# Expert tiles of 128 rows instead of 256, second weight matrices held in SBUF, first ones through four buffers

## The chip, the core and the metric

The kernel runs on one core of a Trainium2 chip, written by hand in Bass: each of the five engines (TensorE "PE", VectorE "DVE", ScalarE "ACT", GpSimd "POOL", SyncE "SP") has its own instruction stream, and semaphores are the only order between them. The metric is the device time of one execution in microseconds (us), lower is better. Arithmetic in the part that is changed is float32, except for the ranking matmuls (bf16 one-hots).

## What is computed

Two Flamingo-style blocks on x of 8 x 512 x 256 and a context of 8 x 1601 x 256. Three parts (a cross attention, an attention with four heads chosen by a router, a cross attention of 16 heads) take nearly all of the time and are not touched. The last part is a mixture of eight experts, of which each row uses one:

```python
x_flat = x.reshape(b * t, d)                      # 4096 rows of 256, normalised
logits = x_flat @ w_gate + b_gate
probs = jax.nn.softmax(logits, axis=-1)
route_p = jnp.max(probs, axis=-1)
route_idx = jnp.argmax(probs, axis=-1)            # one of NE = 8 experts
h = jax.nn.relu(jnp.einsum('nd,edm->enm', x_flat, W1) + b1[:, None, :])   # 256 -> 1024
y = jnp.einsum('enm,emd->end', h, W2) + b2[:, None, :]                    # 1024 -> 256
out = y[route_idx, jnp.arange(n)] * route_p[:, None]
x = x + jnp.tanh(g_ffn[1]) * out
```

## The kernel before

**The first 2900 us.** A software pipeline over the eight batch items; in each, NU = 208 steps `u` place the work of three items on the engines. Each engine's stream is an unrolled loop over `b` and `u` (SP: `attend` and `fill`). The last round, b = B, finishes the last item: heads out, output projection (L1079), norm, gate (L1087). In it SP stores the item's residual (L470), its normalised rows (L474) and its gate weights (L478) to `dramR`, one row of 528 floats per token.

**The routing.** VectorE makes one-hots of the expert numbers, TensorE counts and ranks with small matmuls (L1311, L1314), and VectorE works out how many tiles each expert needs and which expert each tile belongs to: `tex`, ET integers (L1773 to L1783, signal `v_tex`). Then it makes one-hots of tile columns (L1795, `v_oht`, four pieces early and one for the last item's rows after L1801 to L1792), and TensorE multiplies them with one-hots of the ranks (L1322, 64 matmuls, the last eight for the last item) into the list of row numbers per tile (`pe_id`). VectorE turns it into gather and scatter indices (L1807, L1810, `v_id`).

**The expert stage.** The rows are sorted by expert into tiles of TS rows. As each expert's rows are padded to whole tiles, ET = 4096 / TS + 7 tiles are computed, whatever the inputs. NH = TS / 128. For each tile j:
- SP (`load_weights`, L511) waits until tile j - 2 is done (`v_y`), loads the tile's expert number into a register (L515) and issues four DMAs: first matrix (L516, 256 x 1024, 1 MB), first bias (L518), second matrix (L520, 1024 x 256, 1 MB), second bias copied to all partitions (L522). Two buffers of each.
- POOL (`fetch`, L682) gathers the tile's rows from `dramR` with one indirect DMA per 128 rows, XB = 3 tiles ahead.
- TensorE transposes the rows (`turn_rows`, L1334), VectorE copies them to SBUF (`rows_in`, L1815).
- TensorE (`hidden`, L1344) computes the hidden layer transposed: 8 blocks of 128 hidden units by 2 halves of the input; the weights are the stationary operand and the TS rows stream past. One f32 matmul in the code is two instructions in the trace. Results go to PSUM banks 2 to 5 (`h_place`); ScalarE adds bias and ReLU (L883) into `hT`, after a signal per full bank.
- TensorE (`outputs`, L1355) computes the output rows: for each 128 rows, 8 matmuls with `hT` stationary and the second matrix, 256 columns, streaming.
- VectorE (`rows_out`, L1822 and L1823) adds the bias, multiplies with the gate weight and adds the residual; POOL scatters the rows to `dramO` (L692).

TensorE's order is `turn_rows(0)`, then for every j `hidden(j)`, `turn_rows(j + 1)`, `outputs(j)`. At the end SP copies `dramO` to the output (L533).

Of the kernel before, what the change touches and what calls it, by code (L numbers as in the profile page):

```python
# [8 lines left out]
F32 = mybir.dt.float32  # L9
# [3 lines left out]
ALU = mybir.AluOpType  # L13
# [3 lines left out]
B, S, C, D = 8, 512, 1601, 256  # L17
P = 128
QT = S // P
KD = D // P  # L20
CT = -(-C // P)
# [9 lines left out]
GH = 4  # L31
# [12 lines left out]
FM = FF // P  # L44
TOK = B * S
NT = TOK // P
TS = 256
ET = TOK // TS + NE - 1
NH = TS // P
NJ = ET * NH  # L50
TE = NT - QT
RW = 2 * D + 16
XB = 3
MASKED = -float(2.0 ** 100)

MB, F0, F1, F2, SB, VB = (0, 1), 2, 3, 4, (5, 6), 7
# [83 lines left out]
def flamingo(nc, a):  # L140
    ctx_stack = ExitStack()
    with ctx_stack:
        def sem(name):
            return ctx_stack.enter_context(nc.semaphore(name))
# [55 lines left out]
        def carve(region, size):  # L200
            at = [0]

            def take(dims, dt, parts=P):
                n = int(np.prod(dims)) * (4 if dt in (F32, I32, U32) else 2)
                words = -(-n // 4)
                ap = region[0:parts, at[0]:at[0] + words]
                at[0] += words
                assert at[0] <= size, (at[0], size)
                if dt is not F32:
                    ap = ap.bitcast(dt)  # L210
                if dt in (BF16,) and words * 2 != int(np.prod(dims)):
                    ap = ap[:, 0:int(np.prod(dims))]
                names = "abcd"[:len(dims)]
                if len(dims) > 1:
                    ap = ap.rearrange(f"p ({' '.join(names)}) -> p {' '.join(names)}",
                                      **{k: v for k, v in zip(names, dims)})
                return ap
            return take
# [75 lines left out]
        spare = take([1], F32)  # L294

        take = carve(regC, R - R_AB)
        hT = take([FM, TS], F32)
        ys = [take([NH, D], F32) for _ in range(2)]
        w1 = [take([KD, FF], F32) for _ in range(2)]
        w2 = [take([FM, D], F32) for _ in range(2)]  # L300
        b1 = [take([FM], F32) for _ in range(2)]
        b2 = [take([D], F32) for _ in range(2)]
        xs = [take([NH, RW], F32) for _ in range(XB)]
        xsT = [take([KD, TS], F32) for _ in range(2)]

# [41 lines left out]

        g_late, v_oh, pe_rank, v_tex, v_ohr, v_oht, pe_id, v_id = (
            sem(n) for n in ("g_late", "v_oh", "pe_rank", "v_tex", "v_ohr", "v_oht", "pe_id", "v_id"))
        w_loaded = [sem(f"w_loaded{i}") for i in range(2)]  # L350
        xs_loaded = [sem(f"xs_loaded{i}") for i in range(XB)]
        pe_xsT, v_xsT, pe_h, a_h, pe_y, v_y = (sem(n) for n in ("pe_xsT", "v_xsT", "pe_h", "a_h", "pe_y", "v_y"))
        ys_stored = [sem(f"ys_stored{i}") for i in range(2)]
# [8 lines left out]
        def _(sp):  # L362
# [101 lines left out]

            def fill(b, u):
                n, e = b + 1, b - 1
                if e >= 0:
                    if u == 21:
                        sp.wait_ge(v_oC, QT * (e + 1))
                        sp.dma_start(dramR[S * e:S * (e + 1), D:2 * D].rearrange("(t p) n -> p t n", p=P), xc  # L470
                                     ).then_inc(x_stored, 16)
                    if u == 28:
                        sp.wait_ge(v_xn, 4 * norm_d(e) + 4)
                        sp.dma_start(dramR[S * e:S * (e + 1), 0:D].rearrange("(t p) n -> p t n", p=P), xn  # L474
                                     ).then_inc(n_stored, 16)
                    if u == U_GATE + 8:
                        sp.wait_ge(v_wt, e + 1)
                        sp.dma_start(dramR[S * e:S * (e + 1), 2 * D:RW].rearrange("(t p) n -> p t n", p=P), w16[:]  # L478
                                     ).then_inc(w_stored, 16)
                if n < B:  # L480
                    for i in range(VP):
                        if u == U_V[i] + 2:
                            store_v(n, i)
                    if u == U_RL + 4:
                        gather_heads(n)
                    if u == U_QC[0] + 5:
                        store_q(n, 0)
                    if u == U_QC[0] + 8:
                        load_q(n, 0)
                    if u == 153:  # L490
                        store_q(n, 1)
                    for i in range(2 * NCH):
                        if u == U_K[i] + 3:
                            store_k(n, i)
# [14 lines left out]
                                         ).then_inc(ld["ones"], 16)  # L509

            def load_weights(j):  # L511
                par = j % 2
                if j >= 2:
                    sp.wait_ge(v_y, NH * (j - 1))
                e = sp.value_load(tex[0:1, j:j + 1], min_val=0, max_val=NE - 1)  # L515
                sp.dma_start(w1[par], a["D_W1"][bass.ds(e, 1)].rearrange("o (k p) f -> p (o k) f", p=P)  # L516
                             ).then_inc(w_loaded[par], 16)
                sp.dma_start(b1[par], a["D_b1"][bass.ds(e, 1)].rearrange("o p m -> (o p) m")  # L518
                             ).then_inc(w_loaded[par], 16)
                sp.dma_start(w2[par], a["D_W2"][bass.ds(e, 1)].rearrange("o (k p) n -> p (o k) n", p=P)  # L520
                             ).then_inc(w_loaded[par], 16)
                sp.dma_start(b2[par], a["D_b2"][bass.ds(e, 1)].rearrange("o n -> (o n)").partition_broadcast(P)  # L522
                             ).then_inc(w_loaded[par], 16)

            sp.wait_ge(n_stored, 16 * B)
            sp.wait_ge(x_stored, 16 * B)
            sp.wait_ge(v_tex, 1)
            for j in range(ET):
                load_weights(j)
# [178 lines left out]
        def _(act):  # L708
# [166 lines left out]
                        start_next(b + 2, u)  # L875

            def hidden(j):
                par = j % 2
                act.wait_ge(w_loaded[par], 64 * (j // 2 + 1))
                for m in range(FM):  # L880
                    bank, at = h_place(j, m)
                    act.wait_ge(pe_h, HBK * j + m // (FM // HBK) + 1)
                    act.activation(hT[:, m, :], PS[:, bank, at:at + TS], ACT.Relu,  # L883
                                   bias=b1[par][:, m:m + 1]).then_inc(a_h, 1)
# [6 lines left out]
        def _(pe):  # L891
# [421 lines left out]
            for i in range(QT):  # L1313
                last = mm(PS[:, 0, QT * NE:(QT + 1) * NE], onesD, oh[:, TE + i, :], start=i == 0, stop=i == QT - 1)  # L1314
            last.then_inc(pe_rank, 1)
            for i in range(NT):
                if i % 7 == 0 and i < TE:
                    pe.wait_ge(v_oht, i // 7 + 1)
                if i == TE:
                    pe.wait_ge(v_oht, 5)  # L1320
                for k in range(2):
                    last = mm(PS[:, 1, 0:NJ], ohr[k][:, i, :], oht[:, i, :], start=i == 0 and k == 0,  # L1322
                              stop=i == NT - 1 and k == 1)
# [12 lines left out]
                last.then_inc(pe_xsT, 1)  # L1336

            def hidden(j):
                pe.wait_ge(w_loaded[j % 2], 64 * (j // 2 + 1))
                pe.wait_ge(v_xsT, j + 1)  # L1340
                for m in range(FM):
                    bank, at = h_place(j, m)
                    for kk in range(KD):
                        last = mm(PS[:, bank, at:at + TS], w1[j % 2][:, kk, m * P:(m + 1) * P], xsT[j % 2][:, kk, :],  # L1344
                                  start=kk == 0, stop=kk == KD - 1)
                    if (m + 1) % (FM // HBK) == 0:
                        last.then_inc(pe_h, 1)

            def outputs(j):
                for t in range(NH):  # L1350
                    past(pe, v_y, NH * j + t - 1)
                    for m in range(FM):
                        if t == 0:
                            pe.wait_ge(a_h, FM * j + m + 1)
                        last = mm(PS[:, 6 + (NH * j + t) % 2, 0:D], hT[:, m, t * P:(t + 1) * P], w2[j % 2][:, m, :],  # L1355
                                  start=m == 0, stop=m == FM - 1)
                    last.then_inc(pe_y, 1)

            turn_rows(0)
            for j in range(ET):  # L1360
                hidden(j)
# [6 lines left out]
        def _(dve):  # L1368
# [322 lines left out]
            def alone(ins):  # L1691
                ins.then_inc(*own.tick())
                dve.wait_ge(v_self, own.now())
# [123 lines left out]
            def rows_out(j):  # L1817
                par = j % 2
                past(dve, ys_stored[par], 16 * NH * (j // 2))
                for t in range(NH):  # L1820
                    dve.wait_ge(pe_y, NH * j + t + 1)
                    alone(v.tensor_tensor(ys[par][:, t, :], PS[:, 6 + (NH * j + t) % 2, 0:D], b2[par], ALU.add))  # L1822
                    v.scalar_tensor_tensor(out=ys[par][:, t, :], in0=ys[par][:, t, :],  # L1823
                                           scalar=xs[j % XB][:, t, 2 * D:2 * D + 1], in1=xs[j % XB][:, t, D:2 * D],
                                           op0=ALU.mult, op1=ALU.add).then_inc(v_y, 1)
# [64 lines left out]
```

## Time and profile before

| | us |
|---|---|
| median of the runs | 3290.82 |
| lowest and highest of three runs | 3289.27, 3303.54 |
| the profiled execution | 3308.77 |
| its span, first to last instruction | 3307.0 |
| mean granted TensorE clock, share of full | 0.937 |

Rows of the trace give the start of a piece or an instruction in us from the span's start, and its duration. PE is TensorE's matmul, PEld its weight loads, which can run beside matmuls. "xN" is a number of instructions. The duration of a single matmul is counted from start to the modelled end of its pipeline; the distance of two starts tells its pace better. A name with q (SPq, PEldq) is an engine's sequencer.

### The profile page before, as it was taken

To read this page: it belongs to the slowest core of one execution; us is meant where nothing else is said; L and a number is where in the kernel's file an instruction comes from. 1 tells how busy PE (TensorE), PEld (TensorE's weight loads), DVE (VectorE), ACT (ScalarE), POOL (GpSimd) and SP (SyncE) were. 2 spreads that over 40 slices of the span, in tenths; PEclk is the share of its full clock that TensorE was granted. 3 is DMA by queue.
4 is the path that set the end of the run, shared out by engine and by line. 5 is a ranking of instruction groups with operands and counts; after the bars stand their busy time and mean duration, and the time that the engine had idled before them with its cause. 6 is when DMAs were issued, how large, how long until landed. Compare 5 with 4: busy or idle time off the path is not lost.

```text
span 3307.0 us, 38212 instructions
## 1 busy us (share of the span) xinstructions
PE 2877.2 (87%) x13236; PEld 1331.4 (40%) x13236; DVE 1719.2 (52%) x4156; ACT 1459.8 (44%) x2794; POOL 316.6 (10%) x364
## 2 busy tenths in 40 slices
PE   5758988998899888998899889988998888859997
PEld 3423423353334333443344334433343322148886
DVE  1335556556555656555655565555555676621111
ACT  2122454545454555445454545454545555612221
POOL 0110001010100100010101010101010000012221
PEclk7878998999899999999999999998999999969999
DMA  4124212322232214220323032303221121026665
GB/s 156 54 70 110 56 34 77 88 61 50 70 94 55 64 36 119 55 74 28 99 69 80 16 119 62 82 20 119 63 63 33 53 55 36 8 90 220 219 208 175
DMA packets 190687, 267.58 MB, mean 81 GB/s; under 512 B 47813, under 2 KB 159661, under 8 KB 190358
## 3 DMA queue, kind: packets, MB, share of 16 engines
q1 hardware_dynamic: 173084, 189.97, 21.3%
q0 software_dynamic: 17408, 75.13, 6.7%
q8 instruction: 107, 1.75, 0.2%
q14 instruction: 88, 0.72, 0.1%
HBM read 203.24 MB, written 65.61 MB: 81 GB/s over the span
## 4 chain that ended last, share of the span: by engine, by line
PE 72%; DVE 15%; ACT 5%; issue 4%; SPq 3%; DMA 1%; POOL 0%; ACTq 0%; POOLq 0%; DVEq 0%
PE PS L1233 12%; PE PS L1184 10%; DVE mxC L1655 9%; PE PS L1216 7%; PE PS L953 6%; PE PS L929 5%; PE PS L1344 5%; PE PS L1355 5%; PE PS L1019 2%; PE PS L1099 2%; PE PS L1036 2%; PE PS L1029 2%; PE PS L976 2%; DVE nmB L1494 1%; PE PS L940 1%
## 5 line engine op out<-in xcount | busy, mean ns | idle before, releaser
L860 ACT ACTIVATE reg<-PS 128x512 f32<-128x512 f32 (+1 forms) x1664 | 970.3, 598 | 1205.2 <-PE PS L1216 1201.9
L1655 DVE TENSOR_REDUCE mxC<-PS 128x1 f32<-128x400 f32 (+1 forms) x2048 | 1090.1, 569 | 752.9 <-PE PS L1184 743.2
L1184 PE MATMUL PS<-reg 96*128 96x400 bf16 (+1 forms) x2048 | 693.0, 351 | 176.5 <-DVE mxC L1655 155.7
L1216 PE MATMUL PS<-reg 99*128 99x512 bf16 (+1 forms) x1664 | 642.5, 396 | 32.5 <-ACT reg L860 27.1
L1184 PEld LDWEIGHTS PS<-reg 96*128 96x128 bf16 x2048 | 203.1, 99 | 725.0 <-DVE mxC L1655 598.9
L1233 PE MATMUL PS<-reg 128*17 128x512 f32 (+1 forms) x3328 | 461.8, 628 | 0.0
L1216 PEld LDWEIGHTS PS<-reg 99*128 99x128 bf16 (+1 forms) x1664 | 165.6, 102 | 348.5 <-ACT reg L860 159.1
L929 PE MATMUL PS<-reg 128*128 128x512 f32 (+1 forms) x512 | 206.0, 526 | 1.2 <-ACT reg L756 0.7
L883 ACT ACTIVATE reg<-PS,reg 128x256 f32<-128x256 f32 x184 | 77.3, 471 | 271.0 <-PE PS L1344 271.0
L953 PE MATMUL PS<-reg 128*128 128x512 f32 (+1 forms) x416 | 193.1, 598 | 0.4 <-ACT reg L728 0.4
L1344 PE MATMUL PS<-reg 128*128 128x256 f32 x736 | 165.4, 382 | 0.9 <-DVE reg L1815 0.9
L1355 PE MATMUL PS<-reg 128*128 128x256 f32 x736 | 163.3, 379 | 0.0
L1344 PEld LDWEIGHTS PS<-reg 128*128 128x128 f32 x736 | 140.6, 191 | 22.1 <-issue 1.2
L1355 PEld LDWEIGHTS PS<-reg 128*128 128x128 f32 x736 | 137.5, 189 | 19.1
L1029 PE MATMUL PS<-ident,reg 128*128 128x128 f32 x512 | 93.6, 312 | 52.0 <-ACT reg L751 52.0
L929 PEld LDWEIGHTS PS<-reg 128*128 128x128 f32 x512 | 89.6, 195 | 77.5 <-issue 65.6
L559 POOL DMA_DIRECT2D reg<-in_A_mask x32 | 17.9, 562 | 1028.0 <-PE PS L1036 638.5
L1029 PEld LDWEIGHTS PS<-ident,reg 128*128 128x128 f32 x512 | 65.2, 158 | 124.0 <-issue 116.8
L1424 DVE CUSTOM_DVE_ANT_0 reg<-PS,reg 128x512 f32<-128x512 f32 (+1 forms) x128 | 72.4, 568 | 74.0 <-PE PS L929 68.9
L976 PE MATMUL PS<-reg,wkC 128*128 128x400 f32 (+1 forms) x256 | 107.3, 546 | 0.7 <-DVE reg L1486 0.7
L953 PEld LDWEIGHTS PS<-reg 128*128 128x128 f32 (+1 forms) x416 | 78.1, 192 | 73.4 <-issue 67.1
L1494 DVE TENSOR_REDUCE nmB<-PS 128x1 f32<-128x512 f32 x128 | 82.0, 682 | 45.9 <-PE PS L1019 45.9
(202 smaller groups left out, 2614.7 us busy)
## 6 DMA issues: line engine op xcount, KB each, us to landing
reg<-in_D_W SPq DMA_DIRECT2D x46, 1024.0 KB, 7.5
reg<-in_A_mask POOLq DMA_DIRECT2D x32, 800.5 KB, 4.8
dramK<-reg SPq DMA_DIRECT2D x144, 100.0 KB
dramV<-reg SPq DMA_DIRECT2D x48, 272.0 KB, 2.1
reg<-in_ctxT POOLq DMA_DIRECT2D x8, 1601.0 KB, 8.3
reg<-in_ctx POOLq DMA_DIRECT2D x8, 1536.0 KB, 8.1
dramQ<-reg SPq DMA_DIRECT2D x96, 128.0 KB
reg<-dramQ SPq DMA_DIRECT2D x32, 384.0 KB, 5.8
```

Of the source, the lines that this page charges most:

```text
L860: act.activation(pr[u % RING][0:r, :], PS[0:r, s_bank(g, v), :], ACT.Exp).then_inc(a_expC, 1)
L929: last = mm(PS[:, FB[i % 2], 0:w], qgA[:, k, t * P:(t + 1) * P], ctxT[:, k, c0:c0 + w], start=k == 0, stop=k == KD - 1)
L953: last = mm(PS[:, FB[m], :], ctxN[0:r, c, m * P:(m + 1) * P], ptA[0:r, c, :], start=c == 0, stop=c == CT - 1)
L976: last = mm(PS[:, FB[u % 2], 0:w], wkC[:, k, m * P:(m + 1) * P], ctxT[:, k, c0:c0 + w], start=k == 0, stop=k == KD - 1)
L1029: last = tr(PS[:, F2, k * P:(k + 1) * P], pB[i % 4][:, k * P:(k + 1) * P], ident[:])
L1184: last = mm(PS[:, bank, 0:w], qs[(NG * bb + g) % 3][0:ROWS, h, t * P:(t + 1) * P], ks[g % 2][0:ROWS, h, c0:c0 + w], start=True, stop=True)
L1216: last = mm(PS[0:r, bank, :], ks[g % 2][0:STK, h, c * P:c * P + r], qs[(NG * b + g) % 3][0:STK, h, :], start=True, stop=not with_mask)
L1233: last = mm(PS[32 * h:32 * h + DC + 1, VB, :], vc[0:r, c, g * GH + h, :], pr[(UN * g + GH * c + h) % RING][0:r, :], start=c == 0, stop=c = ...
L1344: last = mm(PS[:, bank, at:at + TS], w1[j % 2][:, kk, m * P:(m + 1) * P], xsT[j % 2][:, kk, :], start=kk == 0, stop=kk == KD - 1)
L1355: last = mm(PS[:, 6 + (NH * j + t) % 2, 0:D], hT[:, m, t * P:(t + 1) * P], w2[j % 2][:, m, :], start=m == 0, stop=m == FM - 1)
L1494: v.tensor_reduce(nmB[:, i:i + 1], PS[:, (F0, F1)[h], :], AX.X, ALU.max, negate=True).then_inc(v_nmB, 1)
L1655: v.tensor_reduce(mxC[:, h, t, j:j + 1], PS[:, MB[i % 2], 0:M_CH[j][1]], AX.X, ALU.max).then_inc(v_mx, 1)
```

## The change

- TS goes from 256 to 128: 39 tiles of 128 rows instead of 23 of 256, NH from 2 to 1, one gather and one scatter per tile. XB, the row buffers, goes from 3 to 4.
- The second matrices of all eight experts are loaded into one SBUF tensor with eight 1 MB DMAs. They stand in SP's stream at b = B, u = 6, behind a wait for the last attention product. SP waits for them to land before the first `load_weights`, TensorE before the first `turn_rows`.
- TensorE loads the expert numbers of all 39 tiles into registers, in five calls of up to eight, behind a wait for `v_tex` and ahead of the L1322 matmuls. The matmuls of `outputs` read the second matrix at an address computed from the register.
- First matrices and the two biases go through WB = 4 buffers. `load_weights` waits for tile j - 4 and issues three DMAs; before the third tile's it waits for the rows of the second.

```diff
-TS = 256
+TS = 128
-XB = 3
+XB = 4
+WB = 4
...
         take = carve(regC, R - R_AB)
+        w2 = take([NE, FM, D], F32)
+        assert NE * FM * D <= 2 * GH * C + 3 * GH * S // 2 + RING * S + CT * S // 2
+        w1 = [take([KD, FF], F32) for _ in range(WB)]
         hT = take([FM, TS], F32)
         ys = [take([NH, D], F32) for _ in range(2)]
-        w1 = [take([KD, FF], F32) for _ in range(2)]
-        w2 = [take([FM, D], F32) for _ in range(2)]
-        b1 = [take([FM], F32) for _ in range(2)]
-        b2 = [take([D], F32) for _ in range(2)]
+        b1 = [take([FM], F32) for _ in range(WB)]
+        b2 = [take([D], F32) for _ in range(WB)]
...
             def fill(b, u):
                 n, e = b + 1, b - 1
+                if b == B and u == 6:
+                    sp.wait_ge(pe_pv, UN * B)
+                    for i in range(NE):
+                        sp.dma_start(w2[:, i, :, :], a["D_W2"][i].rearrange("(k p) n -> p k n", p=P)
+                                     ).then_inc(w2_loaded, 16)
...
             def load_weights(j):
-                par = j % 2
-                if j >= 2:
-                    sp.wait_ge(v_y, NH * (j - 1))
+                par = j % WB
+                if j >= WB:
+                    sp.wait_ge(v_y, NH * (j - WB + 1))
+                if j == 2:
+                    sp.wait_ge(xs_loaded[1], 16 * NH)
...
-                sp.dma_start(w2[par], a["D_W2"][bass.ds(e, 1)].rearrange("o (k p) n -> p (o k) n", p=P)
-                             ).then_inc(w_loaded[par], 16)
...
+            sp.wait_ge(w2_loaded, 16 * NE)
             sp.wait_ge(v_tex, 1)
...
             last.then_inc(pe_rank, 1)
+            pe.wait_ge(v_tex, 1)
+            chosen = []
+            for j in range(0, ET, 8):
+                _, some = nc.values_load_multi_w_load_instructions(
+                    tex[0:1, j:min(j + 8, ET)], engines=[mybir.EngineType.PE], min_val=0, max_val=NE - 1,
+                    skip_runtime_bounds_check_because="the vector engine takes the minimum with NE - 1")
+                chosen += some
...
-                        last = mm(PS[:, 6 + (NH * j + t) % 2, 0:D], hT[:, m, t * P:(t + 1) * P], w2[j % 2][:, m, :],
+                        last = mm(PS[:, 6 + (NH * j + t) % 2, 0:D], hT[:, m, t * P:(t + 1) * P],
+                                  w2[:, bass.ds(chosen[j], 1), m, :].rearrange("p o n -> p (o n)"),
                                   start=m == 0, stop=m == FM - 1)
                     last.then_inc(pe_y, 1)
 
+            pe.wait_ge(w2_loaded, 16 * NE)
             turn_rows(0)
```

## Rows read from the trace of the kernel before

**Rows 1.** The page's first line.

```profile
span 3307.0 us, 38212 instructions
```

**Rows 2.** Windows: from, to, length, busy time by engine, clock, DMA share, GB/s.

```profile
3000.00:3050.00 50.00, 50.00 (x238) 43.70 (x237) 8.45 (x17) 12.18 (x30) 15.01 (x16) 1.00 0.62 201
```

**Rows 3.** Chain that ended last, expert stage: start us, us, what.

```profile
2954.25 1.13 PE PS L1334 x4
2956.24 9.21 PE PS L1344 x32
...
3001.43 6.93 PE PS L1344 x32
3008.80 6.94 PE PS L1355 x32
3015.74 6.93 PE PS L1344 x32
...
3280.30 3.48 PE PS L1355 x16
```

**Rows 4.** Timeline of TensorE around one tile's transposes.

```profile
3251.53 0.60 PE L1334 MATMUL PS<-ident,reg 128*128 128x128 f32 x4
3251.96 0.82 PE L1355 MATMUL PS<-reg 128*128 128x256 f32 x3
```

**Rows 5.** The same chain, a gate of an earlier item, at full clock.

```profile
2738.56 1.69 PE PS L1087 x16
```

**Rows 6.** Groups by line and shape: count, busy us, mean ns, idle before.

```profile
L883 ACT ACTIVATE reg<-PS,reg 128x256 f32<-128x256 f32 x184 | 77.3, 471 | 271.0 <-PE PS L1344 271.0
L1815 DVE COPY reg<-PS 128x512 f32<-128x512 f32 x23 | 15.9, 692 | 154.0 <-PE PS L1334 154.0
```

**Rows 7.** Timeline of the hand-over, from the routing to the first gather.

```profile
2936.27 0.35 DVE L1780 TENSOR_TENSOR reg<-reg 128x184 f32<-128x184 f32 x1
...
2937.03 0.18 DVE L1783 TENSOR_SCALAR reg<-reg 128x23 int32<-128x23 f32 x1
...
2938.25 0.40 SPq L516 DMA_DIRECT2D reg<-in_D_W  x1
...
2938.93 2.33 PE L1322 MATMUL PS<-reg 128*128 128x46 bf16 x56 [4.26 <-DVE reg L1795]
...
2941.08 0.38 SPq L516 DMA_DIRECT2D reg<-in_D_W  x1
...
2944.76 0.49 PE L1322 MATMUL PS<-reg 128*128 128x46 bf16 x8 [3.49 <-DVE reg L1795]
...
2946.43 1.10 POOL L682 DMA_INDIRECT reg<-dramR,reg  x1 [23.53 <-DVE reg L1810]
```

**Rows 8.** Timeline, last attention products and last store.

```profile
2899.85 1.92 PE L1233 MATMUL PS<-reg 128*17 128x512 f32 x16
...
2934.01 0.36 SPq L478 DMA_DIRECT2D dramR<-w  x1
```

**Rows 9.** Windows, columns as rows 2, while loads and gathers fill the DMA engines.

```profile
2950.00:2955.00 5.00, 0.75 (x4) 0.71 (x4) 0.00 (x0) 0.00 (x0) 2.88 (x4) 0.50 1.07 373
```

**Rows 10.** DMA issues, KB each, median us to landing (two stretches, 2860 to 2975 and 3000 to 3200).

```profile
dramR<-reg SPq DMA_DIRECT2D x2, 512.0 KB, 3.0
...
dramO<-reg POOLq DMA_INDIRECT x29, 2.7
reg<-dramR,reg POOLq DMA_INDIRECT x28, 6.8
```

**Rows 11.** Sequencer instructions of two lines: duration ns min, median, max.

```profile
L1299 PEldq TENSOR_LOAD <-mflag x1: 487/487/487, 248.2 to 248.2; - x1
L1299 PEldq FUSED_REGOPS  x1: 168/168/168, 248.8 to 248.8; - x1
...
L516 SPq FUSED_REGOPS  x19: 42/42/42, 3003.3 to 3260.6; - x19
```

**Rows 12.** Timeline of TensorE at that register load.

```profile
248.23 3.78 PE L916 MATMUL PS<-reg,gA 128*128 128x512 f32 x4 [0.69 <-ACT reg L714]
```

More of the change, by code:

```diff
@@ L349, in flamingo @@
             sem(n) for n in ("g_late", "v_oh", "pe_rank", "v_tex", "v_ohr", "v_oht", "pe_id", "v_id"))
-        w_loaded = [sem(f"w_loaded{i}") for i in range(2)]
+        w_loaded = [sem(f"w_loaded{i}") for i in range(WB)]
+        w2_loaded = sem("w2_loaded")
         xs_loaded = [sem(f"xs_loaded{i}") for i in range(XB)]
@@ L877, in hidden @@
             def hidden(j):
-                par = j % 2
-                act.wait_ge(w_loaded[par], 64 * (j // 2 + 1))
+                par = j % WB
+                act.wait_ge(w_loaded[par], 48 * (j // WB + 1))
                 for m in range(FM):
@@ L1338, in hidden @@
             def hidden(j):
-                pe.wait_ge(w_loaded[j % 2], 64 * (j // 2 + 1))
+                pe.wait_ge(w_loaded[j % WB], 48 * (j // WB + 1))
                 pe.wait_ge(v_xsT, j + 1)
@@ L1343, in hidden @@
                     for kk in range(KD):
-                        last = mm(PS[:, bank, at:at + TS], w1[j % 2][:, kk, m * P:(m + 1) * P], xsT[j % 2][:, kk, :],
+                        last = mm(PS[:, bank, at:at + TS], w1[j % WB][:, kk, m * P:(m + 1) * P], xsT[j % 2][:, kk, :],
                                   start=kk == 0, stop=kk == KD - 1)
@@ L1821, in rows_out @@
                     dve.wait_ge(pe_y, NH * j + t + 1)
-                    alone(v.tensor_tensor(ys[par][:, t, :], PS[:, 6 + (NH * j + t) % 2, 0:D], b2[par], ALU.add))
+                    alone(v.tensor_tensor(ys[par][:, t, :], PS[:, 6 + (NH * j + t) % 2, 0:D], b2[j % WB], ALU.add))
                     v.scalar_tensor_tensor(out=ys[par][:, t, :], in0=ys[par][:, t, :],
```

## The prediction

> **What bounds the kernel now.** I read the page first. One core runs for 3307.0 us [rows 1]. The windows come next: outside the last stage the three engines share the work, while in the expert stage TensorE is busy for all of each 50 us at granted clock 1.00 (the 2.4 GHz level), VectorE for 8.45, ScalarE for 12.18, and the DMA engines for 0.62 of their time at 201 GB/s [rows 2]. Only this stage and the hand-over before it are touched, so the 2900 us before it stay. Third, the chain that ended last. From the first tile to the last output it is TensorE alone, 32 first-layer instructions in 6.93 us, then 32 second-layer ones in 6.94, and one tile follows the other after 3015.74 - 3001.43 = 14.31 us [rows 3]. The small gap behind the first layer is the transposes of the next tile's rows. 23 such tiles make 329 us, near the stage's own 3280.30 + 6.94 - 2956.24 = 331.0 (the chain's last piece leaves TensorE halfway); the other 2 us are the first tile, whose first layer took 9.21 us behind a slow-clock stretch [rows 3]. Fewer TensorE columns here shorten the kernel one for one, as long as nothing else becomes the limit.
>
> **Smaller tiles.** Rows are padded to whole tiles per expert, and the worst case is computed always: 23 tiles of 256 rows (5888) become 32 + 7 = 39 of 128 (4992). An f32 matmul is two instructions here (16 in the code, 32 in the row).
> - Second layer: same shape per instruction (stationary 128x128, moving 256), 16 per tile instead of 32. 6.94 / 32 = 0.217 us each, so 16 take 3.47.
> - First layer: still 32 instructions a tile, each with 128 moving columns instead of 256, and each still with its own weight load. This is the price that decides. Half the columns give 0.108 us. The weight load must then fit beside it: the gate's 16 instructions of 8 columns, which can hardly be anything but weight loads, take 1.69 us, 0.106 each [rows 5]. Whether load and stream overlap at 128 columns is seen at the transposes: four of 128x128 start 3251.53, and the next layer starts 3251.96, 0.43 us for four, 0.108 each, with their loads in it [rows 4]. So 32 x 0.108 = 3.47 us.
> - Transposes: two instead of four, 0.22.
> A tile takes 3.47 + 3.47 + 0.22 = 7.16 us, and 39 take 279.2 against 329.0: **-49.8 us**.
>
> That rests on overlap. The Trainium skill ("TensorE: Matmul & The Clock Gate", Back-to-back issue gap) says that a stream of load and matmul pairs runs slower than the isolated gap where the moving side is short, 81 ns against 56 at 128 columns. The transposes here don't show that. By its ratio, 1.45, the first layer would take 5.0 us, and the sum for the tiles would be +10 instead of -50.
>
> **What must hide behind 7.16 us.** ScalarE: eight ReLUs a tile at 0.471 us for 256 columns [rows 6]; even at that price 3.8 us, and the first four can start when half the first layer is done, 1.7 us before TensorE is through it; TensorE asks for the fifth 1.7 us into the second layer. I cost it at nothing. VectorE: a copy of half the columns that took 0.692 us [rows 6] and two operations on 256 columns, under 2 us. POOL: one gather and one scatter, some 1 us each, as often per row as before. Gathers land in 6.8 us and scatters in 2.7 [rows 10]; a gather is issued some 15 us ahead, a scatter has two tiles (14 us). DMA: per tile 1.05 MB first matrix, 0.13 MB bias rows, 0.27 MB gathered, 0.13 scattered, 1.58 MB in 7.16 us = 221 GB/s, where a stretch of this trace moves 373 [rows 9]. The second matrix, a third of the old bytes, is gone from the loop, so this stays covered; if it fell to 186 GB/s the tile would be 8.5 us and the loop's gain zero. SP took 2941.08 - 2938.25 = 2.83 us for a register load and four DMAs [rows 7]; three are less, and they wait only for the tile four back, a lead of three tiles.
>
> **Second matrices loaded once.** Eight 1 MB DMAs are put in SP's queue after the last attention product, which ends at 2899.85 + 1.92 = 2901.8 [rows 8], ahead of SP's three stores of the last batch, of which the last is issued at 2934.01 [rows 8]. DMA is idle meanwhile. 8.4 MB at 373 GB/s is 22.5 us: landed by about 2925. The two earlier stores (issued near 2920 and 2924) may queue a few us; nobody needs them before the gather at 2946.43 [rows 7]. The other bound is the rate of one 512 KB store, 0.52 MB in 3.0 us, 175 GB/s [rows 10]: 48 us, landed at 2950. SP now waits for it before the first expert load, now at 2938.25 [rows 7], and TensorE before the first tile, so that would cost about 5 to 8 us. I take the first (many large transfers in flight, like the stretch of rows 9) and cost it at nothing.
>
> **Register loads.** TensorE now reads 39 expert numbers, in five calls of up to eight, between the tile table (L1783, ready 2937.03 + 0.18 = 2937.21) and the 64 ranking matmuls, queued right behind. These wait for VectorE: 56 start at 2938.93 and take 2.33 us, and the last eight can't start before 2944.76 [rows 7]. So 2944.76 - 2937.21 - 2.33 = 5.2 us are free. One load of one value on TensorE took 0.487 us, and its arithmetic 0.168 [rows 11]. Ends: 5 x 0.487 = 2.4 us (nothing on the path) and 39 x 0.655 = 25.5 (20 us on the path). I take five calls and no cost, but keep the other end. The skill's page "Runtime: NRT & Kernel Launch" (Instruction fetch mechanics) gives some 200 ns per register even in bulk; 39 would be 7.8 us and the sum 2.6 us worse; no row here shows a bulk load.
>
> **Computed addresses.** Each second-layer matmul may need register instructions on TensorE's sequencer; SP's take 0.042 us before a DMA, the one on TensorE took 0.168 [rows 11]. One or two of them per matmul are 0.04 to 0.34 us, beside 2 x 0.217 = 0.434 us of matmul. The sequencer ran that one at 248.8, while matmuls that began at 248.23 ran on for 3.78 us [rows 12], so it works beside them: nothing.
>
> **The hand-over.** VectorE's table operations get wider: L1780 took 0.35 us for 184 columns [rows 7] and gets 312, its neighbour L1774 gets 256 for 128. Four such operations widen by some 0.1 us each (an estimate, less than in proportion), and the narrower one-hots give part back: +0.2. Then it gets better. Before, the first two gathers shared the engines with four 1 MB loads and TensorE began at 2954.25, 7.8 us after POOL. Now only 2.4 MB are ahead, done about 2946, the third load waits for the second gather, and the first tile needs one gather. With the scatters' 2.7 us [rows 10] and POOL's 1, it starts 3.5 us after POOL: about -4.4 with the 0.2 in it. Two transposes and a half-size copy save 0.6 of the 1.99 us up to the first layer. Together **-4.8 us**. If contention stays, this is only -1.
>
> **Sum**: -49.8 - 4.8 = -54.6. The tail after the last output is unchanged. The profiled execution took 3308.77 us (span plus 1.8), 18 above the median 3290.82 of the runs, so 3254 for that one and **3236 us** by the median.
>
> **Rivals.**
> A. TensorE's register loads are serial, each of 39 at full price: the ranking is late by up to 20 us. For: only a single-value load is in the trace, at 0.487. Against: five calls. 3236 + 20 = 3256. If both this and the slow second-matrix load hold, 3262. Chance 0.14.
> B. Slower than before: the sequencer can't feed the second layer. Place: the eight matmuls of each tile; price: four or more register instructions of 0.168 before each, 0.67 us, plus waits that keep it from running ahead. From 0.434 + 54.6 / 312 = 0.61 us per matmul on the change loses. At 0.434 + 0.24 the time is 3236 + 75 = 3311. For: no such matmul is in the trace. Against: 0.042 on SP, and run-ahead at 248.8. Chance 0.05.
> C. Load and stream don't overlap fully at 128 columns: if half of the 0.106 us load stays outside, 39 x 32 x 0.053 = 66 us more, 3302, no difference that can be told (all of it outside would be 3368). For: only four such instructions stand in a row anywhere. Against: their 0.108 [rows 4]. Chance 0.05. The ratio of the skill's page named above would put it at 3296.
> D. Part of either, 0.12 us per first-layer instruction or a stall of some 0.4 us per tile (ReLU late, register work): 3236 + 16 = 3252. Chance 0.14.
> Forecast: 0.62.
>
> **Numbers.** Range 3222 to 3266: down for a faster load of the second matrices or a spread of the runs, up to hold A, and D with the 13 us by which the slowest run shown lies above the median; outside are B and C. A measurement tells 0.5%, 16 us, from no change. Faster 0.90 (forecast, A, D), same 0.05 (C), slower 0.05 (B).
>
> **What would show it.** The chain should have pieces of 3.47 us x32 and x16, tile spacing 7.16; second-layer spacing above 0.217 is B, first-layer above 0.11 is C. L1322's last eight should still start near 2945 (else A); the first tile near 2950; the second matrices landed before 2934; DMA share near 0.6 and no wait for w1 or rows. A loop at 7.16 with an equal total would mean the start-up went wrong.

## The result, and the profile after

| | before | after |
|---|---|---|
| median of 4 runs, us | 3292.14 | 3251.07 |
| lowest and highest, us | 3289.27, 3303.54 | 3246.73, 3263.43 |
| span of the profiled execution, us | 3307.0 | 3261.7 |
| store of the gate weights to first layer of the first tile, us | 22.2 | 21.9 |
| first layer of the first tile to the end, us | 350.8 | 305.1 |

The changed kernel takes 0.9875 of the time of before, 95% interval 0.9839 to 0.9911: 41 us less, clear of noise, and inside the predicted 3222 to 3266, but 15 us above the 3236 that was expected. The last two rows of the table tell more than the medians. The 2900 us ahead of the change carry the same code and still differ by up to 21 us between executions (SP's store of the gate weights is issued between 2913.9 and 2934.7 us in the traces of this study). So stages are measured here from the issue of that store ([rows 8], 2934.01 before) to the end of the span: 373.0 us before, 327.0 after, 326.8 in a second profile of the changed kernel. By this measure the change is worth 46.0 us. The two profiles of the changed kernel agree within 0.2; the kernel before was profiled once.

The expert stage, the chain that ended last (answers to [rows 3]):

```profile
2956.65 5.95 PE PS L1360 x32
2962.82 3.47 PE PS L1371 x16
2966.29 3.57 PE PS L1360 x32
2970.07 3.47 PE PS L1371 x16
2973.55 3.57 PE PS L1360 x32
...
3227.64 3.57 PE PS L1360 x32
```

L1360 is the first layer, L1371 the second. A tile follows the other after 2973.55 - 2966.29 = 7.26 us, where 7.16 was expected. The second layer is exact. The first takes 3.57 instead of 3.47. Nothing stands between the pieces but the 0.22 us of the transposes.

The hand-over, from SP's loads of the kept matrices to the first tile (timeline, answers to [rows 7, 8]):

```profile
2900.55 1.91 PE L1242 MATMUL PS<-reg 128*17 128x512 f32 x16
...
2902.58 17.40 SPq L473 DMA_DIRECT2D reg<-in_D_W  x8
...
2934.72 0.36 SPq L486 DMA_DIRECT2D dramR<-w  x1
...
2938.27 0.18 DVE L1801 TENSOR_SCALAR reg<-reg 128x39 int32<-128x39 f32 x1
...
2945.40 0.32 DVE L1813 TENSOR_TENSOR reg<-reg 128x156 bf16<-128x156 f32 x1
...
2948.25 2.29 PE L1338 MATMUL PS<-reg 128*128 128x39 bf16 x64 [12.88 <-issue]
...
2951.73 1.10 POOL L691 DMA_INDIRECT reg<-dramR,reg  x1 [28.12 <-DVE reg L1828]
...
2955.38 0.66 PE L1350 MATMUL PS<-ident,reg 128*128 128x128 f32 x2 [4.83 <-DMA reg<-dramR,reg]
```

The reader is to see three things. The eight loads are issued in 17.4 us and delay nothing that anyone waits for; from the end of the last attention product (2900.55 + 1.91) to the store of the gate weights it is 32.3 us, before it was 32.2. The 64 ranking matmuls (L1338) no longer run as 56 and 8 behind VectorE: all start at 2948.25, with "issue" as what ended the idle time, 2.5 us after VectorE's last one-hots were there (2945.40 + 0.32). And from POOL's first gather to the first transposes it is 3.65 us; it was 7.8 before [rows 3, 7]. What held the ranking is TensorE's sequencer (rows of L1328, ns, and where the first and the last start):

```profile
L1328 PEldq TENSOR_LOAD <-reg x5: 1702/1930/1951, 2938.5 to 2946.5; - x5
```

Five bulk loads one behind the other, 1.93 us for eight values and 1.70 for seven: 0.24 us a value. From 2938.5 to 2946.5 + 1.7 = 2948.2 TensorE started no matmul.

Windows of the expert stage (answers to [rows 2]):

```profile
3000.00:3050.00 50.00, 50.00 (x348) 46.99 (x348) 8.96 (x21) 15.15 (x54) 13.71 (x14) 1.00 0.66 219
```

TensorE is busy for all of it, at the same granted clock of 1.00, and the DMA engines move 219 GB/s where 221 was worked out.

### The profile page after: what moved, and what is told of

Its sections match the earlier page's. It is cut to its first block, busy times and chain, and to the rows that moved or that the text cites. A ratio compares the mean times of both kernels' runs of the same rounds, so it can differ in the third digit from the quotient of the medians.

```text
span 3261.7 us, 39651 instructions
## 1 busy us (share of the span) xinstructions
PE 2831.2 (87%) x13622; PEld 1308.7 (40%) x13622; DVE 1714.2 (53%) x4158; ACT 1469.5 (45%) x2922; POOL 302.7 (9%) x350
## 3 DMA queue, kind: packets, MB, share of 16 engines
q1 hardware_dynamic: 166444, 193.18, 21.9%
## 4 chain that ended last, share of the span: by engine, by line
PE 71%; DVE 15%; ACT 5%; issue 4%; SPq 3%; DMA 1%; POOL 0%; ACTq 0%; POOLq 0%; DVEq 0%
PE PS L1242 12%; PE PS L1193 10%; DVE mxC L1673 9%; PE PS L1225 7%; PE PS L962 6%; PE PS L938 5%; PE PS L1360 4%; PE PS L1371 4%; PE PS L1028 2%; PE PS L1108 2%; PE PS L1045 2%; PE PS L1038 2%; PE PS L985 2%; DVE nmB L1512 1%; PE PS L949 1%
## 5 line engine op out<-in xcount | busy, mean ns | idle before, releaser
L892 ACT ACTIVATE reg<-PS,reg 128x128 f32<-128x128 f32 x312 | 89.0, 368 | 217.0 <-PE PS L1360 217.0
L1360 PEld LDWEIGHTS PS<-reg 128*128 128x128 f32 x1248 | 147.4, 194 | 3.1 <-issue 1.0
L1360 PE MATMUL PS<-reg 128*128 128x128 f32 x1248 | 147.8, 277 | 0.6 <-DVE reg L1833 0.6
L1371 PE MATMUL PS<-reg 128*128 x624 | 141.7, 379 | 0.0
L1371 PEld LDWEIGHTS PS<-reg 128*128 128x128 f32 x624 | 115.1, 189 | 15.1
L938 PEld LDWEIGHTS PS<-reg 128*128 128x128 f32 x512 | 89.3, 194 | 77.0 <-issue 65.0
L568 POOL DMA_DIRECT2D reg<-in_A_mask x32 | 17.9, 562 | 1026.8 <-PE PS L1045 635.7
```

The lines of the kernel that those rows point to most:

```text
L938: last = mm(PS[:, FB[i % 2], 0:w], qgA[:, k, t * P:(t + 1) * P], ctxT[:, k, c0:c0 + w], start=k == 0, stop=k == KD - 1)
L1360: last = mm(PS[:, bank, at:at + TS], w1[j % WB][:, kk, m * P:(m + 1) * P], xsT[j % 2][:, kk, :], start=kk == 0, stop=kk == KD - 1)
```

## The experiments

Where a ratio stands the run was timed against the kernel before; all are compared by stage. The columns are us of the profiled execution, and "store to end" is the measure above. Each kernel but the changed one was profiled once, and the four without a ratio (fixed address, two buffers, no wait for the second gather, tile size alone) were run only for that profile.

| run | store to first layer | first layer to end | store to end |
|---|---|---|---|
| before | 22.2 | 350.8 | 373.0 |
| changed kernel | 21.9 | 305.1 | 327.0 |
| late loads | 17.9 | 307.8 | 325.7 |
| fixed address, no register loads | 17.7 | 305.6 | 323.2 |
| small tiles, all weights streamed, four buffers | 21.0 | 305.4 | 326.4 |
| kept matrices, tiles of 256 | 20.3 | 349.2 | 369.4 |
| two buffers | 21.8 | 333.5 | 355.3 |
| no wait for the second gather | 24.2 | 305.2 | 329.4 |
| loads by four | 18.1 | 305.4 | 323.5 |
| tile size alone | 21.1 | 434.9 | 455.9 |
| streamed, wait for the first gather | 17.5 | 306.8 | 324.3 |

**The changed kernel once more.**

> The changed kernel once more, as the yardstick of this chip. Expected: ratio near 0.9875, tiles 7.26 us apart, ranking matmuls 2.5 us or so after VectorE's last one-hots, first layer 54.2 us after the end of the last attention product.

Ratio 0.9889 (0.9855 to 0.9923), tiles 7.26 us apart, first layer 21.90 us after the store. The stages repeat to 0.2 us; the medians don't, to 5.

**What the register loads cost: loads placed later.**

```diff
-            for j in range(0, ET, 8):
+            def choose(j):
...
             pe.wait_ge(w2_loaded, 16 * NE)
+            choose(0)
             turn_rows(0)
             for j in range(ET):
                 hidden(j)
                 if j + 1 < ET:
                     turn_rows(j + 1)
+                if j and j % 8 == 0:
+                    choose(j)
                 outputs(j)
```

> The expert numbers are loaded into TensorE's registers later: the first eight after the ranking matmuls, while the first gather is on its way, the others eight at a time between first and second layer of tiles 8, 16, 24 and 32. Theory (the five bulk loads of 1.9 us stood in front of the ranking and pushed it back 4.3 us, and the sequencer can load registers while the array works off queued matmuls): first layer about 50 us after the last attention product instead of 54.2, tile pace unchanged at 7.26, total 4 us less than the changed kernel (ratio to the kernel before about 0.986). Rival (a load stalls the array wherever it stands): 4 us won at the start, and 4 x 1.9 = 7.7 us given back in the loop, total 3 us more than the changed kernel. Rival (the start is bound by the gather behind the weights, not by the ranking): no change.

Both the theory and half of the rival came true. The first layer starts 4.1 us earlier, so the loads had been on the path, which refutes "the start is bound by the gather". But from the first layer to the end it is 2.8 us longer, with four waits at the second layer (waits of TensorE, then the second layer of tile 8 in the chain):

```profile
PE PS L1373 <- ACT reg L892: 1.6, 4, 0.5
```

```profile
3009.83 3.73 PE PS L1373 x16
```

The columns of the first are total, times and longest, us. The waits are put down to ScalarE, whose first four ReLUs were done at 3008.6; what ended last there is the load, which started at 3007.2 and took some 2.3 us. A second layer behind such a wait also takes 3.73 us instead of 3.47. Together the four loads push the tiles back by 0.74, 0.69, 0.74 and 0.48 us, 2.65 in all (distances of the starts of second layers), and the first tile's first layer adds 0.3, 6.28 us against 5.95. That is the 2.8 within 0.2. The rival had four times 1.9 us. Ratio 0.9854 (0.9811 to 0.9898): no difference from the changed kernel that the timed runs can tell; the stages give 1.3 us.

**Do computed addresses cost anything?**

```diff
-                                  w2[:, bass.ds(chosen[j], 1), m, :].rearrange("p o n -> p (o n)"),
+                                  w2[:, j % NE, m, :],
```

and the register loads are gone. So the tiles don't take the second matrix of their expert, and the output is not the reference's; the work of each tile is the same.

> No register loads on TensorE at all, and the second layer reads the second matrix of expert j modulo 8 at a fixed address, so the output differs from the reference in which second matrix a tile uses. Theory (computed addresses cost nothing, the 0.1115 us of a first-layer instruction is the array's own pace): second layer 0.217 us and first layer 0.1115 us per instruction as in the changed kernel, first layer starts about 50 us after the last attention product. Rival (register work slows the loop): first layer back at 0.108 us, tile 7.16 us, 4 us less in the loop on top of the start.

The chain of this kernel (L1354 first layer, L1344 transposes, L1365 second layer):

```profile
3101.22 3.47 PE PS L1365 x16
3104.69 3.57 PE PS L1354 x32
3108.26 0.22 PE PS L1344 x2
3108.48 3.47 PE PS L1365 x16
```

Still 7.26 us, to the hundredth. Computed addresses cost nothing, and the 0.1 us of the first layer is not register work. Without any register load the first tile starts 4.2 us earlier; its first layer takes 6.39 us instead of 5.95, which leaves 3.8 us.

**The tile size, with all weights streamed through four buffers.** Both matrices are loaded for each tile, w2 in four buffers like w1; no kept matrices, no registers. SP's wait for the second gather before the third tile's loads stays.

```diff
+        w2 = [take([FM, D], F32) for _ in range(WB)]
...
+                sp.dma_start(w2[par], a["D_W2"][bass.ds(e, 1)].rearrange("o (k p) n -> p (o k) n", p=P)
+                             ).then_inc(w_loaded[par], 16)
...
+                                  w2[j % WB][:, m, :],
```

> Tiles of 128 rows and four buffers, but both matrices of a tile are loaded for it, as before; nothing is kept, no registers on TensorE. Per tile 2.63 MB. Theory (DMA would have become the limit, which is what the kept matrices are for): at the 348 GB/s at which the eight kept matrices were loaded, 7.56 us a tile, TensorE waits for weights, loop 295 us instead of 285, and the first layer starts some 4 us later than with an undisturbed gather; total 5 to 20 us above the changed kernel. Rival (the prefetch over four tiles is enough, kept matrices bring nothing): tiles 7.26 us apart, total that of the changed kernel or 4 us less, since the register loads are gone.

The theory falls, and the rival is right. Windows of this kernel, from, to, length, busy by engine, clock, DMA share, GB/s:

```profile
3000.00:3050.00 50.00, 50.00 (x348) 47.01 (x347) 9.35 (x21) 16.01 (x56) 13.71 (x14) 1.00 1.05 364
3100.00:3150.00 50.00, 50.00 (x346) 46.93 (x346) 9.16 (x21) 15.67 (x55) 13.30 (x14) 1.00 1.05 367
```

The DMA engines are busy for the whole stage, at 356 to 367 GB/s in the four windows from 3000 to 3200, and TensorE never waits for weights: 2.63 MB in 7.26 us is 362 GB/s. So in the loop, with four buffers, the kept matrices bring nothing. 362 is what the loop asks for and not quite what the engines can give: with the same bytes per tile the last run below moves 373 to 375. At the start the kept matrices save the first gather from waiting behind 4 MB of weights (TensorE's idle time, L1339 transposes):

```profile
2939.44 0.69 PE L1339 MATMUL PS<-ident,reg 128*128 128x128 f32 x2 [8.21 <-DMA reg<-dramR,reg]
```

From POOL's gather at 2932.41 to these it is 7.0 us against 3.65, and that is about what the register loads cost on the other side. Ratio 0.9872 (0.9842 to 0.9902): the time of the changed kernel.

**Kept matrices, tiles of 256 rows.**

```diff
-TS = 128
+TS = 256
-XB = 4
+XB = 3
```

> Second matrices kept and four buffers, but tiles of 256 rows as before (23 tiles, three bulk register loads). Theory (the loop is bound by TensorE's columns, all of the gain is the tile size): tiles 14.3 us apart, loop 331 us as before; three loads take 5.7 us against 5.2 free, so the start is 0 to 4 us better than before through the undisturbed gather; ratio 0.998 to 1.001. Rival (part of the gain is the saved weight traffic): loop shorter than 331 us.

Ratio 0.9989 (0.9970 to 1.0009), no difference. The loop has its old pace:

```profile
2961.28 6.93 PE PS L1360 x32
2968.65 6.94 PE PS L1371 x32
2975.59 6.93 PE PS L1360 x32
```

So the kept matrices and the four buffers give nothing in the loop at this tile size. By the stages the kernel is 3.6 us better than before. 2.0 are at the start: from POOL's first gather to the first transposes it is 5.5 us (2937.89 to 2943.39) instead of 7.8, and the three register loads (5.6 us) make that gather 0.4 us later. 0.7 more are the first layer of the first tile, 8.56 us against 9.21, and the rest is behind the last product. The other 42.4 us of the 46.0 come only with the small tiles.

**Two buffers instead of four.**

```diff
-WB = 4
+WB = 2
...
-                if j == 2:
-                    sp.wait_ge(xs_loaded[1], 16 * NH)
```

> As the changed kernel, with two instead of four buffers for first matrices and biases, and without SP's wait for the second gather (with two buffers it would come before a wait that holds it anyway). Theory: the load for a tile is issued about 1.8 us after the tile before last ends and lands 5.5 us later, 7.3 us against a tile of 7.26, so TensorE waits up to 1 us at each first layer: tile 7.3 to 8.2 us, loop 3 to 35 us longer. Rival (one tile of lead is enough): tile 7.26 us and the same time.

28 us slower than with four, near the upper end of the 3 to 35 that were expected. TensorE waits 26 times for 21.2 us in all, and a first layer behind such a wait takes 3.84 us instead of 3.57. One turn of its chain:

```profile
3103.86 3.48 PE PS L1369 x16
3107.44 0.43 DVE reg L1838
3107.90 0.50 DVE reg L1839
...
3109.15 0.39 SPq L524
3109.72 0.69 SPq L526
3110.59 5.27 DMA reg<-in_D_b
3115.90 3.84 PE PS L1358 x32
```

The way from the end of a tile (3107.34) over VectorE and SP's three issues to the landing of the last small load (3115.86) is 8.5 us, longer than the 7.26 us of the tile between. With tiles of 256 the same way had 14.3 us.

**The tile size alone.** The streamed kernel with two buffers. Four row buffers (XB) stay, where the kernel before has three; no run tells what that is worth.

```diff
-WB = 4
+WB = 2
...
-                if j == 2:
-                    sp.wait_ge(xs_loaded[1], 16 * NH)
```

> Tiles of 128 rows and nothing else: both matrices of a tile are loaded for it, through two buffers as before. Theory (the lead of two buffers is the issue: a buffer is free 2 us after the tile before last, four DMAs are issued in about 1.6 us and land 7.4 to 9.5 us later, so 11 to 13 us from the end of tile j - 2 to the start of tile j, and two tiles take that plus 7.26): 9.2 to 10.2 us a tile, loop 360 to 400 us, 30 to 60 us slower than the kernel before. Rival (DMA throughput is enough, so the buffers hardly matter): 7.3 to 7.8 us a tile.

83 us slower than before by the stages; the one execution took 3381.41 us. The mechanism is the expected one, the size was underrated (9.2 to 10.2 us a tile and 30 to 60 us in all were expected). One turn of the chain:

```profile
3119.86 3.48 PE PS L1358 x16
3123.43 0.44 DVE reg L1826
3123.89 0.50 DVE reg L1827
...
3126.12 0.38 SPq L522
3126.68 8.06 DMA reg<-in_D_b
3134.78 5.33 PE PS L1347 x32
3140.33 3.48 PE PS L1358 x16
3143.91 0.44 DVE reg L1826
```

Two tiles take 20.5 us here (3119.86 to 3140.33); over the stage pairs take 20.4 to 23.5, 21.4 in the mean, 10.7 a tile. From the end of a tile (3123.34) to landed weights (3134.74) it is 11.4 us, of which TensorE spends 7.3 on the tile between. Then it stands still (waits of TensorE):

```profile
PE PS L1347 <- DMA reg<-in_D_b: 89.6, 20, 6.1
```

The part that was not expected is the first layer's 5.33 us instead of 3.57. The granted clock of these stretches shows its cause (windows, columns as [rows 2]: the wait, the 3 us behind it, the next 2 us):

```profile
3130.60:3134.70 4.10, 0.00 (x0) 0.00 (x0) 0.91 (x2) 0.00 (x0) 1.96 (x2) 0.98 1.04 324
3134.80:3137.80 3.00, 3.00 (x14) 3.00 (x15) 0.00 (x0) 0.00 (x0) 0.00 (x0) 0.50 1.02 399
3138.00:3140.00 2.00, 2.00 (x20) 2.00 (x20) 0.00 (x0) 1.14 (x4) 0.00 (x0) 1.00 1.06 361
```

After a stand-still of 4.2 us (3130.6 to 3134.8) the first layer begins at 0.50, the 1.2 GHz level, 14 instructions in 3 us, and is back at 1.00 from 3138.0 on, 20 in 2 us. First layers behind a wait take 5.27 to 6.75 us, 5.7 in the mean of the 18 in the chain. So the 129.5 us that two buffers cost here against four are 89.6 of waits and, for nearly all of the rest, slow clock behind them: 20 x 2.1 = 42 by the mean (an estimate, 2 us more than is there).

**The wait for the second gather.** Four tiles' weights issued at once.

```diff
-                if j == 2:
-                    sp.wait_ge(xs_loaded[1], 16 * NH)
```

> As the changed kernel, without SP's wait for the second gather before the third tile's weights, so that four 1 MB loads are issued at once. Theory (the first gather is held up by bulk loads in the DMA queues): from POOL's first gather to the first transposes 3.65 us becomes 5 to 8 us, total 2 to 4 us more. Since the register loads have moved POOL's gather 4 us back, most of the four loads may be through by then; then only 0 to 1 us more. Rival (gathers don't suffer from loads): 3.65 us stays.

```profile
2949.73 0.66 PE L1348 MATMUL PS<-ident,reg 128*128 128x128 f32 x2 [6.97 <-DMA reg<-dramR,reg]
```

From POOL's gather at 2943.94 it is 5.8 us instead of 3.65, the first layer 2.2 us later, and 2.4 us more to the end. The gather does suffer, and the wait in the change is worth 2.2 us. The 0 to 1 us that the expectation held possible, should the loads be through by then, did not come.

**Loads by four.** As the late loads, with the calls of four values before the second layer of every fourth tile.

> As the late loads, but four expert numbers at a time, before the second layer of every fourth tile. The late loads by eight left waits of 0.4 us at four tiles and, with a slower first tile, 2.8 us more from the first layer to the end. Theory (a load of four takes about 1 us and fits into what the sequencer is ahead of the array): no wait in the loop; from the store of the gate weights to the end 323.5 us, against 326.8 to 327.0 in the changed kernel. Rival (each load costs the array some 0.4 us whatever its size): nine loads, 3.6 us, so 327.

Store to end 323.5 us, TensorE's only waits after the ranking are those for the first gather and the first copy, and the loads took this:

```profile
L1329 PEldq TENSOR_LOAD <-reg x10: 767/1000/1017, 2925.0 to 3197.8; - x10
```

1.0 us is hidden where 2.3 us (the loads of eight in the loop) was not. Ratio to before 0.9873 (0.9841 to 0.9905). It is 3.5 us better than the changed kernel by the stages, which is too little for the timed runs to show.

**Streamed, with a wait for the first gather.**

```diff
-                if j == 2:
-                    sp.wait_ge(xs_loaded[1], 16 * NH)
+                if j == 1:
+                    sp.wait_ge(xs_loaded[0], 16 * NH)
```

> Both matrices loaded for every tile through four buffers, without register loads, and SP waits for the first gather before the second tile's loads. Theory (kept matrices are worth only the undisturbed first gather, and this wait gives it too): first layer 18 to 19 us after the store of the gate weights instead of 21.0, and if the DMA engines, full at 363 GB/s in the streamed version, catch up, 323 to 324 us from that store to the end. Rival (there is no slack in the DMA engines, so a later start of the second tile's weights comes back as waits of TensorE): some 5 us of waits in the first ten tiles, 327 us or more.

The first layer starts 17.5 us after the store, and the later weights cost one wait of 0.8 us (waits of TensorE, then a window as above):

```profile
PE PS L1349 <- DMA reg<-in_D_b: 0.8, 1, 0.8
```

```profile
3100.00:3150.00 50.00, 50.00 (x348) 47.03 (x347) 9.36 (x21) 16.02 (x56) 13.71 (x14) 1.00 1.06 374
```

Both numbers are just outside what the theory gave, 18 to 19 and 323 to 324 us. 324.3 us from store to end, ratio 0.9840 (0.9794 to 0.9886). Without kept matrices and registers this kernel is as fast as the changed one, or 2.7 us faster. Its DMA engines are busy throughout. They move 373 to 375 GB/s from 3000 to 3150, where the loop asks for 362, so the spare is some 3% (an estimate from the two).

## Why the prediction was right, and where it was off

- **Tiles, -49.8 us.** Measured 350.8 - 305.1 = 45.7. The mechanism is the predicted one: 39 tiles, TensorE alone, no wait. The mis-sized term is the first layer's instruction, 0.1115 us, not 0.108: 39 x 32 x 0.003 = 4 us is the whole difference. I took half of the 0.217 us of 256 columns. A third width in the trace of before shows that this couldn't be exact, six instructions of 512 columns at clock 1.00:

```profile
339.23 2.58 PE PS L953 x6
```

That is 0.430 each. With the 0.217 of 256 columns it gives 0.833 ns per column and 0.003 us that don't shrink, so 0.110 at 128 (an estimate). That is the pace of the transposes (0.44 us for four, 0.22 for two in the chains) and half of the miss, some 2 us, which rows at hand could have told. In [rows 4] the four transposes, read to 0.01 us, are between 0.105 and 0.11 each: below the first layer's pace, so they were no measure of it. The other 1.5 ns of a first-layer instruction are open. The fixed address run excludes register work as their cause; that a small part of the weight load (0.106 us alone) stays outside the stream is not excluded.
- **Rival C and the page behind it.** Load and stream overlap at 128 columns almost fully. The prediction's sign for C was a first layer above 0.11; it came, barely, with 4 us behind it and not 66, so the sign was drawn too tight. The Trainium skill ("TensorE: Matmul & The Clock Gate", Back-to-back issue gap) has 81 ns for a pair at this width against 56 isolated, a ratio of 1.45. The trace doesn't agree for these f32 instructions: 0.1115 against half of 0.217 is a ratio of 1.03.
- **Hand-over, -4.8 us.** Measured -0.3. The gain at the gather was there, 4.15 us (3.65 against 7.8), and the smaller first tile gave 0.7 (2955.38 to 2956.65 is 1.27 against 1.99). VectorE's wider table operations cost 0.5 and the narrower one-hots gave 0.2 back, 0.3 for the 0.2. The step that failed is the register loads "at no cost". The ends (2.4 to 25.5 us) held what came, and I took the low one; five calls took 9.7 us, since a call costs 0.24 us per value and not 0.487 per call. Only 5.2 us were free. All 64 ranking matmuls then had to run behind them. They ended at 2948.25 + 2.29 = 2950.5, where eight of 0.5 us behind the last one-hots would have ended at 2946.2: some 4.3 us. By the prediction's own sign (the last eight near 2945) this was rival A. Rival A held in part, at a fifth of its 20 us. The gather term is also added up a little wrong: 7.8 - 3.5 is 4.3, less 0.2 is 4.1 and not 4.4, and with the 0.6 the sum is 4.7. The Trainium skill ("Runtime: NRT & Kernel Launch", Instruction fetch mechanics) gives some 200 ns per register even in bulk. The measured 0.24 us is near it; by its figure the sum would have been 2.6 us worse (an estimate), more than half of the 4.5 by which the hand-over missed.
- **Kept matrices at no cost.** Right: 348 GB/s where 373 was taken, landed some 26 us after the first issue (the last is issued at 2917.1 and lands 11.9 us later at most). The two stores behind them land 10.1 and 6.9 us after their issue instead of some 3, and nothing waits for them.
- **Computed addresses, rival B.** The register instruction before a matmul takes 0.046 us on TensorE's sequencer and runs beside the work; excluded by the fixed address run.

```profile
L1371 PEldq FUSED_REGOPS  x217: 46/46/60, 3000.1 to 3196.1; - x109
```

- **DMA.** I named the smaller traffic as what keeps the loop covered. The streamed run shows that this was not needed. What was needed, and what I had passed over in a clause, is the lead of four buffers: with two, the same tiles cost 28 us more with kept matrices and 129 us more without. So the kept matrices do save time where the buffers are too few, 101 us with two, and none with four.
- **The rest of the distance.** Of the 15 us between 3236 and 3251, the tiles are 4.1 and the hand-over 4.5. The median of before moved by 1.3, from 3290.82 to 3292.14. The last 5 are the difference between 41 us by the medians and 46 by the stages. The interval of the ratio, 29 to 53 us, holds both; that it is the spread of the code ahead of the change is likely, not shown. That the median fell inside the range needed no luck: both misses together are under 9 us.

## What to carry to other kernels

Smaller tiles pay for padding saved only if the way from a freed buffer to landed weights (here 8.5 to 11.4 us) fits into the tiles between, so deepen the buffers in the same change; deeper buffers did here what the saved traffic was thought to do. The waits of 4.5 us here cost half as much again in the slow clock behind them, those of 0.8 us didn't. Price a bulk register load per value, keep it away from what others wait for, and split it into pieces shorter than the work that is queued. When you halve a matmul's columns, take the part that doesn't shrink from two widths that the trace has, and leave room for more: here it told half of the miss.

## What the runs showed of the hardware

- A register load on TensorE's sequencer took 1.0 us for four values, 1.93 for eight between idle engines, 2.3 for eight in the loop.
- The DMA engines carried 356 to 367 GB/s in windows of 50 us of the streamed kernel beside a TensorE that never waited, with gathers and scatters (6.6 and 6.0 us to landing) between; 373 to 375 for 150 us in the one that waits for the first gather.
- A gather of 128 rows took 3.65 us from POOL's start to the transposes with two 1 MB loads issued 10 to 12 us before it, 5.8 with four issued 4.5 to 12 us before it, 7.0 with four issued 4 to 8 us before it.
- With waits of 4.5 us on average ahead of every second tile the granted clock was 0.50 behind the wait (for 3.0 us in the turn shown) and 0.84 to 0.93 over windows of 50 us, and the first layer behind a wait took 5.3 to 6.75 us instead of 3.57. The waits of 0.8 us on average with two buffers and kept matrices left the clock at 1.00, and the first layer behind one took 3.84.
- f32 instructions with 128x128 stationary at clock 1.00: 0.430 us with 512 moving columns, 0.217 with 256, 0.1115 with 128 in the first layer and 0.110 in transposes.
